# The reciprocal root of a layer norm as one power on GpSimd, and the product with it there too

## The reference, cut to what matters

```python
WIDTH, LAYERS, M1, M2 = (32, 4, 12, 12)
def layer_norm(x, g, b):
    mu = jnp.mean(x, axis=-1, keepdims=True)
    var = jnp.mean((x - mu) ** 2, axis=-1, keepdims=True)
    return (x - mu) * jax.lax.rsqrt(var + EPS) * g + b
h = layer_norm(x @ fc0_w + fc0_b, ln0_g, ln0_b)
for i in range(LAYERS):
    x1 = spectral_conv(h, w1, w2)        # 2-D FFT, 24 x 12 modes mixed over channels, inverse FFT
    x2 = jnp.einsum('bchw,oc->bohw', h, conv_w[i]) + conv_b[i][None, :, None, None]
    h = layer_norm(x1 + x2, ln_g[i], ln_b[i])
    if i < LAYERS - 1:
        h = gelu(h)
h = gelu(h @ fc1_w + fc1_b)
h = gelu(h @ fc2_w + fc2_b)
h = h @ fc3_w + fc3_b
```

## Time and profile before

| | |
|---|---|
| runs | 3285.81, 3277.0, 3279.34 us; median 3279.34 |
| span of the profiled execution | 3279.2 us (an own total of that execution is not listed) |
| TensorE busy | 2937.9 us, 90% of the span |
| VectorE busy | 2145.9 us, 65% |
| ScalarE busy | 1950.3 us, 59% |
| GpSimd busy | 61.9 us, 2% |
| chain that ended last | TensorE 79%, VectorE 11%, issue 5%, ScalarE 5% |
| costliest group of VectorE | reduction of line 1624, 397.0 us in 320 |
| product of line 1638 | 386.8 us in 320 |

### The profile page before, as it was taken

The page is one execution under the profiler, slowest core; times in us unless marked ns, Lnnn a source line. Parts: engine busy times, 40 slices in busy tenths (PEclk is TensorE's granted clock), DMA queues, the critical chain, the costliest instruction groups (busy, mean ns, idle before and its releaser), DMA issues.

```text
span 3279.2 us, 82177 instructions
## 1 busy us (share of the span) xinstructions
PE 2937.9 (90%) x32240; PEld 1867.7 (57%) x32240; DVE 2145.9 (65%) x3954; ACT 1950.3 (59%) x2271; POOL 61.9 (2%) x81
## 2 busy tenths in 40 slices
PE   7888889999889999889999889999999987964994
PEld 3545466666666666666666544444444447952893
DVE  6888668888668888668888644454445434255457
ACT  6777656666556666556666457777777753422451
POOL 0000000000000000000000010000000001000000
PEclk9999999999999999999999999999999998986897
DMA  3422346544447544546544423111111000000000
GB/s 96 130 97 99 100 152 209 193 165 164 152 130 218 183 164 163 155 154 209 179 165 164 151 67 86 46 55 58 46 46 55 29 1 1 1 1 0 1 1 13
DMA packets 98093, 335.91 MB, mean 102 GB/s; under 512 B 29928, under 2 KB 61960, under 8 KB 62088
## 3 DMA queue, kind: packets, MB, share of 16 engines
q1 hardware_dynamic: 75400, 161.50, 16.4%
q10 hardware_dynamic: 18432, 134.23, 10.0%
q0 software_dynamic: 4096, 37.75, 5.3%
HBM read 179.29 MB, written 154.14 MB: 102 GB/s over the span
## 4 chain that ended last, share of the span: by engine, by line
PE 79%; DVE 11%; issue 5%; ACT 5%; DVEq 0%; SPq 0%; DMA 0%; ACTq 0%
PE pA L1291 15%; PE pA L1299 8%; PE pT L1385 8%; PE pT L1317 5%; PE pS L1328 5%; PE pD L1342 4%; PE pD L1374 4%; PE pD L1356 4%; PE pD L467 3%; PE pA L467 3%; PE pD L1263 3%; PE pA L1281 3%; PE pS L459 2%; PE pT L459 2%; DVE arena L1657 2%
## 5 line engine op out<-in xcount | busy, mean ns | idle before, releaser
L1624 DVE TENSOR_REDUCE small<-arena 128x32 f32<-128x1056 f32 x320 | 397.0, 1241 | 316.0 <-ACT arena L1461 311.3
L1291 PEld LDWEIGHTS pA<-conv_bd,h_in 128*128 128x128 f32 x4096 | 479.0, 192 | 109.4 <-issue 92.7
L1291 PE MATMUL pA<-conv_bd,h_in 128*128 128x128 f32 x4096 | 517.4, 280 | 8.6 <-DVE arena L1617 2.9
L1451 ACT COPY w_sb<-pA 128x1024 f32<-128x1024 f32 x256 | 259.8, 1015 | 393.0 <-PE pA L1299 343.3
L1638 DVE SCALAR_TENSOR_TENSOR w_sb<-w_sb,small 128x1024 f32<-128x1024 f32 x320 | 386.8, 1213 | 5.5
L1472 ACT ACTIVATE h_new<-pT,bet,gam 128x1024 f32<-128x1024 f32 x256 | 307.5, 1201 | 100.2 <-PE pT L1317 92.1
L1461 ACT ACTIVATE arena<-w_sb 128x1024 f32<-128x1024 f32 x320 | 339.3, 1060 | 13.4
L1317 PEld LDWEIGHTS pT<-cst,w_sb 128*128 128x128 f32 x2048 | 225.2, 143 | 144.5 <-issue 123.9
L1317 PE MATMUL pT<-cst,w_sb 128*128 128x128 f32 x2048 | 283.0, 282 | 23.2 <-DVE w_sb L1638 23.2
L1476 ACT COPY h_rows<-pS 128x1024 f32<-128x1024 f32 x256 | 257.1, 1004 | 64.9 <-PE pS L1328 64.6
L1328 PEld LDWEIGHTS pS<-cst,h_new 128*128 128x128 f32 x2048 | 228.5, 143 | 113.0 <-issue 71.6
(11 more groups left out here) (299 smaller groups left out, 3903.0 us busy)
## 6 DMA issues: line engine op xcount, KB each, us to landing
h_scratch<-h_new ACTq DMA_DIRECT2D x128, 1024.0 KB, 4.5
h_in<-h_scratch SPq DMA_DIRECT2D x128, 1024.0 KB, 5.1
y_scratch<-w_sb POOLq DMA_DIRECT2D x32, 576.0 KB, 8.4
y_in<-y_scratch SPq DMA_DIRECT2D x512, 36.0 KB
w_sb<-in_L_tok_w1r_dram POOLq DMA_DIRECT2D x8, 576.0 KB, 7.0
w_sb<-in_L_tok_w1i_dram POOLq DMA_DIRECT2D x8, 576.0 KB, 6.7
w_sb<-in_L_tok_w2r_dram POOLq DMA_DIRECT2D x8, 576.0 KB, 8.3
w_sb<-in_L_tok_w2i_dram POOLq DMA_DIRECT2D x8, 576.0 KB, 7.7
```

The lines of the kernel that those rows point to most:

```text
L1291: pe.matmul(pA[:, c:c + 128], h_in[:, 1024 * n + c:1024 * n + c + 128], conv_bd[:], start=(j == 0), stop=False, skip_group_check=True)
L1624: dve.reduce_sum(var[n], sq[n % 2], axis=AX).then_inc(s["summed"], 1)
```

## The change

The seven instructions of `root` go. GpSimd gets `rs` and `scale`: one power of `var` to -0.5 (the exponent is a tensor that holds -0.5 in every place), and one product. Both stand in a new string `POOL` of each stage, in the order of the units, and leave the VectorE strings; nothing else in the strings moves. GpSimd's program is rebuilt so that it follows the bodies: the weight loads, the stores of `y` and the copy into `conv_bd` stand between whole bodies. The clearing of `spec` is cut into two halves, after bodies 2 and 3 of stage last, that of `XT` comes after body 4, and SyncE's `token_params` moves from before group 2 to before group 5 of that stage and waits for both halves. `alone` adds one to a semaphore that nothing waits for.

```diff
@@ ORDER, stage first @@
-        "DVE": ("red.3- rs.3- scale.3- cen.0 cen.1 cen.2 red.0 rs.0 scale.0 red.1 f1.0- rs.1 f1.1- red.2 scale.1 "
-                "f2.0- rs.2 f2.1- scale.2"),
+        "DVE": ("red.3- cen.0 cen.1 cen.2 red.0 red.1 f1.0- f1.1- red.2 f2.0- f2.1-"),
+        "POOL": ("rs.3- scale.3- rs.0 scale.0 rs.1 scale.1 rs.2 scale.2"),
@@ ORDER, stage mid @@
-        "DVE": ("red.3- i1.0 rs.3- scale.3- cen.0 cen.1 i1.1 red.0 rs.0 scale.0 red.1 rs.1 f1.1- scale.1 red.2 f1.0- "
-                "rs.2 f2.0- cen.2 scale.2 f2.1-"),
+        "DVE": ("red.3- i1.0 cen.0 cen.1 i1.1 red.0 red.1 f1.1- red.2 f1.0- f2.0- cen.2 f2.1-"),
+        "POOL": ("rs.3- scale.3- rs.0 scale.0 rs.1 scale.1 rs.2 scale.2"),
@@ ORDER, stage last @@
-        "DVE": ("rs.2- scale.2- turn.1- i1.1 red.3- turn.2- rs.3- scale.3- i1.0 turn.3- red.0 red.1 rs.0 rs.1 red.2 "
-                "scale.0 scale.1 turn.0"),
+        "DVE": ("turn.1- i1.1 red.3- turn.2- i1.0 turn.3- red.0 red.1 red.2 turn.0"),
+        "POOL": ("rs.2- scale.2- rs.3- scale.3- rs.0 scale.0 rs.1 scale.1"),
...
-                def rs(h, g):
-
-                    dve.wait_ge(s["summed"], at("summed", ph, L, g, 1 * h + 1))
-                    alone(dve)
-                    c = slice(32 * h, 32 * h + 32)
-                    root(dve, small[:, 128:256][:, c], small[:, 0:128][:, c], root_x, root_u, s["root_chain"], s["rooted"])
-
-                def scale(n, g):
-
-                    dve.wait_ge(s["rooted"], at("rooted", ph, L, g, n // 1 + 1))
-                    z = raw[n].rearrange("p (x o) -> p x o", x=32)
-                    r = rstd[n].rearrange("p (x o) -> p x o", o=1)
-                    dve.scalar_tensor_tensor(out=z, in0=z, scalar=ROOT_SCALE, in1=r.broadcast_to([P, 32, C]),
-                                             op0=ALU.mult, op1=ALU.mult).then_inc(s["normed"], 1)
...
+            pool.memset(minus_half, -0.5).then_inc(s["halves_set"], 1)
...
+                def rs(n, g):
+
+                    if first_group(g) and ph == "first" and n == 0:
+                        pool.wait_ge(s["halves_set"], 1)
+                    pool.wait_ge(s["summed"], at("summed", ph, L, g, n + 1))
+                    alone(pool)
+                    pool.tensor_tensor(rstd[n], var[n], minus_half, ALU.pow).then_inc(s["rooted"], 1)
+
+                def scale(n, g):
+
+                    pool.wait_ge(s["rooted"], at("rooted", ph, L, g, n + 1))
+                    alone(pool)
+                    z = raw[n].rearrange("p (x o) -> p x o", x=32)
+                    r = rstd[n].rearrange("p (x o) -> p x o", o=1)
+                    pool.tensor_tensor(z, z, r.broadcast_to([P, 32, C]), ALU.mult).then_inc(s["normed"], 1)
...
+            def layer(ph, L, do, prepared):
+
+                bodies(ph, do, 1, 2)
+                if ph == "first":
+                    weights(0, 0, 0)
+                    bodies(ph, do, 2, 3)
+                    weights(0, 0, 1)
+                    bodies(ph, do, 3, 4)
+                    weights(0, 1, 0)
+                    bodies(ph, do, 4, 5)
+                    weights(0, 1, 1)
+                    bodies(ph, do, 5, 5 + 10)
+                else:
+                    mixed(L, 1)
+                    weights(prepared, 0, 0)
+                    bodies(ph, do, 2, 3)
+                    weights(prepared, 0, 1)
+                    bodies(ph, do, 3, 5)
                     y_store(L, 1)
...
+                    bodies(ph, do, 5, 6)
+                    weights(prepared, 1, 0)
+                    bodies(ph, do, 6, 7)
+                    weights(prepared, 1, 1)
+                    bodies(ph, do, 7, 15)
+                y_store(prepared, 0)
+                bodies(ph, do, NG - 1, NG)
+                channel_weights(prepared)
...
+            body("into_last", bound(last, 0), bound(here, NG - 1))
+            bodies("last", last, 1, 2)
+            y_store(LAYERS - 1, 1)
+            bodies("last", last, 2, 3)
+            half = at_col[0] // 2
+            pool.memset(spec[:, 0:half], 0.0).then_inc(s["par_cleared"], 1)
+            bodies("last", last, 3, 4)
+            pool.memset(spec[:, half:at_col[0]], 0.0).then_inc(s["par_cleared"], 1)
+            bodies("last", last, 4, 5)
+            pool.wait_ge(s["normed"], at("normed", "last", LAYERS - 1, 4, 2))
             pool.memset(XT[64:128, :], 0.0).then_inc(s["ones_set"], 1)
...
+            bodies("last", last, 5, NG)
+            body("last", None, bound(last, NG - 1))
             token_pool(pool)
```

More of the change, by code:

```diff
@@ L162 @@
                 "mix.0 fc1.0 fc1.1"),
-        "DVE": ("red.3- i1.1 rs.3- scale.3- i1.0 red.0 rs.0 scale.0 red.1 rs.1 f1.1- scale.1 red.2 f1.0- f2.0- f2.1- "
-                "mix.0 turn.0"),
+        "DVE": ("red.3- i1.1 i1.0 red.0 red.1 f1.1- red.2 f1.0- f2.0- f2.1- mix.0 turn.0"),
+        "POOL": ("rs.3- scale.3- rs.0 scale.0 rs.1 scale.1"),
     },
@@ L1144, in y_store, with steps, mixed, channel_weights @@
                         pool.dma_start(dst, src).then_inc(s["y_stored"], 16)
[L1146 to L1152, removed]
+            def steps(p):
+                ph, L = p.ph, p.L
+                def rs(n, g):
[6 more added lines that the diff above has]
+                    pool.wait_ge(s["rooted"], at("rooted", ph, L, g, n + 1))
+                    alone(pool)
+                    z = raw[n].rearrange("p (x o) -> p x o", x=32)
+                    r = rstd[n].rearrange("p (x o) -> p x o", o=1)
+                    pool.tensor_tensor(z, z, r.broadcast_to([P, 32, C]), ALU.mult).then_inc(s["normed"], 1)
+                return dict(rs=rs, scale=scale)
+            def mixed(L, half):
+                n = 2 * L + half
+                pool.wait_ge(s["mix_a_free"], 3 * n + 3)
+                alone(pool)
+                pool.wait_ge(s["mix_b_free"], 3 * n + 3)
+                alone(pool)
+            def channel_weights(L):
+                if isinstance(L, int) and L == 0:
                     pool.wait_ge(s["conv_chain"], 2)
@@ L1171, in _, with body @@
[L1171 to L1174, removed]
+                    alone(pool)
+                pool.tensor_copy(conv_bd[:], conv_all[:, bass.ds(P * L, P)]).then_inc(s["conv_ready"], 1)
+            def body(order, early, late):
+                for op, n, is_late in parse(ORDER[order]["POOL"]):
+                    do = late if is_late else early
+                    if do:
+                        do[op](n)
@@ new lines, in bound, with bodies @@
+            def bound(do, g):
+                return {op: (lambda n, f=f: f(n, g)) for op, f in do.items()}
+            def bodies(ph, do, first, last):
+                if last - first == 1:
+                    body(ph, bound(do, first), bound(do, first - 1))
+                else:
+                    with pool.Fori(first, last) as b:
+                        body(ph, bound(do, b), bound(do, b - 1))
+            def layer(ph, L, do, prepared):
[9 more added lines that the diff above has]
+                    bodies(ph, do, 5, 5 + 10)
+                else:
+                    mixed(L, 1)
[3 more added lines that the diff above has]
+                    bodies(ph, do, 3, 5)
+                    y_store(L, 1)
+                    bodies(ph, do, 5, 6)
[6 more added lines that the diff above has]
+                channel_weights(prepared)
@@ new lines, in _ @@
+            make = lambda ph, L: steps(Phase(ph, L))
+            first = make("first", 0)
+            body("first", bound(first, 0), None)
+            layer("first", 0, first, 0)
+            body("mid", bound(make("mid", 0), 0), bound(first, NG - 1))
+            with pool.Fori(0, LAYERS - 2) as L:
+                here = make("mid", L)
+                layer("mid", L, here, L + 1)
+                body("mid", bound(make("mid", L + 1), 0), bound(here, NG - 1))
+            L = LAYERS - 2
+            here, last = make("mid", L), make("last", LAYERS - 1)
@@ L1658, in f2 @@
                                   bank.rearrange("p (t n) -> p t n", t=2)[:, :, 0:384]).then_inc(s["d_free"], 1)
[L1660 removed]
+                return dict(cen=cen, i1=i1, red=red, turn=turn, f1=f1, f2=f2)
             phases(dve, "DVE", mix, steps, conv_centre, centring)
```

47 lines of the change are left out of this document (9 added, 38 removed).

## The result

The changed kernel takes **3,660 us** (median; 3,652 to 3,668) where the kernel before takes 3,281.6 (the median of four runs): a ratio of 1.115, with a 95% interval of 1.113 to 1.117. The prediction was 3,266 us, its range ended at 3,325. It is wrong in sign and in size: 378 us slower.

What follows compares the result with a forecast made beforehand. TensorE was taken as the bound, with its waits for VectorE's product to be won. Gains of 8.4 us (first stage) and 4.7 (middle), 13.1 together, off 3,279.2 gave 3,266 us; range 3,256 to 3,325.

Steps and rivals of the forecast that it cites:

- the price p of the power: Time of one GpSimd power over 32 elements a partition, on the path from red to turn: taken as 1.0 us.
- the high bound "from rows": For the power: VectorE's seven root instructions, 1.33 us, times the engines' ratio on a product, 1.88, giving 2.5 us.
- The slower rival: A long power makes the turns wait in first and middle stages: at p = 3.0, 32 us slower, 3,311; chance 0.30.
- Its price formula: Each of 15 first bodies loses p - 1.06, each of some 45 middle ones p - 2.65, against the gain of 13.1 us.
- The gain of a body: First stage: TensorE's turn.2- and a later transpose wait less, 0.56 us a body; middle bodies with centring: 0.13 us.
- The 13.1 us of the sum: Whole saving claimed: 8.4 us in the first stage plus 4.7 us in the middle stage, off 3,279.2.
- the 4.7 us of the middle stages: Middle stage: 36 bodies with centring, each 0.13 us shorter with a lighter VectorE.
- The queues, put at 0: GpSimd's queue: moved y stores, weight loads, conv_bd copy, clears and parameter loads, each taken to cost 0.
- the sign of late weights: Sign that the forecast is wrong: VectorE idle in front of cen.0 at each layer's third body.
- The store of y that I looked at: The y store's four issues stand before rs.3-, whose turn.3- comes five TensorE operations later: cost 0.
- The port: VectorE with two SBUF inputs and GpSimd reading SBUF exclude each other; charged nothing, by that rule 3,281; chance 0.10.
- The rival's form of it: With a power of 1.3 us or more, cen.2 holds scale.3- up, 14.6 us in 12 bodies: about 3,281; chance 0.10.

Runs made afterwards that it cites:

- The halved run: The changed kernel with the power on 16 of the 32 columns, the other roots left at 1.0: 3,298.8 us, ratio 1.0055.
- With p at 0.24: The changed kernel with the power replaced by a product of two constant tiles of the same shape: 3,273.5 us, ratio 0.9969.
- the run with the product alone: The changed kernel with the root back as VectorE's seven instructions, only the product on GpSimd, the root's scale in the squares: 3,288.1 us, ratio 1.0019.

## Why the prediction was wrong

**The step that failed is the price p of the power.** I took 1.0 us and called 2.5 the high bound "from rows". It is 5.43. The bound came from VectorE's seven instructions times the ratio of the engines on a product, so it took for granted that a power is a handful of products. The halved run shows 158 ns an element against 1.9 for the product, over 80 times as much. My other argument, that "one instruction pays its start once", is true and beside the point: the start is 0.38 us. The text said that no row excludes a power in long loops, and then gave that 15% and left it out of the range. With nothing in the trace about an operation, the ratio of other operations is no bound.

**The slower rival had the mechanism, not the size.** It named the place, and its last sentence, that above 3.3 us four units no longer fit a first body, is what happened: 29.9 us against 23.9. Its price formula would give 15 x 4.37 + 45 x 2.78 - 13.1, some 178 us, at p = 5.43. Measured are 382 between the spans. It charged one late unit a body; the runs show all four serial on one engine, and TensorE at the lower clock after many of its stands (125.8 us of the 382).

**The gain of a body was right, the total in part by luck.** With p at 0.24 nine first bodies took 209.2 us instead of 215.3, 0.67 less each (0.56 predicted), and the middle ones fell by the predicted 0.13. The 13.1 us of the sum correspond to a ratio of 0.996, at the edge of the measured interval. But the same run holds two terms that I had put at 0 and that nearly cancel: the first body of the last stage takes 68.26 us instead of 75.31, the second 56.08 instead of 46.96. And the 4.7 us of the middle stages do not show in their sum, 1,362.0 us against 1,360.1 between the first and last red.0 of each; the bodies with the mixes vary by more than that.

**Smaller terms.** The product: 1.91 us, not 2.27; half of one long product of another kind was an over-estimate by a fifth. Red's end to GpSimd's start is 0.18, not 0.24, and power to product 0.18, not 0.1. The last stage's bodies: unchanged in the ten of the table, right, but not in three of the five before them. The first is shorter, with the clears moved out of it. The second waits for the store of y (next paragraph). In the fifth the two clears of XT, 3.51 us each, which I had put at 0, stand on GpSimd in front of a power, and a turn stands 3.71 us for the product behind it; with the power left out the same body takes 47.07 us.

**The queues, put at 0, were not 0.** The loads of the weights, "0 to 2 us a layer", cost 8.8 us in the first stage of the run with the product alone, where the middle stage makes up for most of its own. In the changed kernel VectorE stood 39.1 us in 4 waits before cen.0 for them, the sign of late weights that the prediction names. The store of y that I looked at was the one before turn.3-; the one that hurts is the last, whose landing ScalarE's first fin.0 needs: 8.5 us. I asked who stands behind these DMAs in the queue, not who waits for their landing.

**The port.** I wrote that the rows of before say nothing against running both engines at once. They do, between the first two red.0 of the last stage: 5.97 us instead of 0.18, beside a clear. I had looked beside the one product of 4.54 us only. The Trainium skill's rule that I quoted, VectorE with two SBUF inputs against a GpSimd that reads, agrees with the 1.90 us of line 200. Beside a power, which reads two tensors as well, only one half of it shows. With the power alone on GpSimd, 26 powers that start 0.26 us into a product of VectorE take 6.24 us instead of 5.43, most of the 0.95 us that the product still runs. But in the changed kernel 45 of the 48 cen.2 start during a power and take 0.91 to 1.02 us, where the earlier trace rows has 0.96: a power that started first does not hold them. And the rule does not cover the clear, which reads nothing, nor cen.1 in the changed kernel, a TENSOR_SCALAR of 0.24 us that took 1.06 beside a product. The same section of the Trainium skill ("SBUF — State Buffer", "Who interferes with whom") lists tensor_scalar among the operations that can, when their operands allow it, take both ports of VectorE and so collide with GpSimd; these rows agree. The rival's form of it, cen.2 holding up the product, was not put to the test: in no trace does a product start while cen.2 runs, and none took longer than 1.93 us.

## What to carry to other kernels

An operation that no row shows has no price until it is measured alone: give its long case a chance and a place in the range, above all when the cover is a few microseconds. When work moves to an idle engine, add up the whole body there, all units in a row, and not only one unit's path. And of each DMA that changes its place in a queue, ask who waits for its landing, a stage later too.

## What the runs showed of the hardware

A GpSimd power of two f32 tensors costs 158 ns for each element of a partition (from 16 and 32 of them), and 0.24 us is what a product of the same 128x32 costs. A clear on GpSimd can hold a small VectorE instruction to its own end (0.18 us to 5.97). A power does not do the same to an instruction with two SBUF inputs that starts after it (0.91 to 1.02 us beside powers of 5.43), though it is held itself by such a product that has started before it (6.24 us instead of 5.43). TensorE ran the same eight transposes in 1.97 us, at a granted clock of 0.50, after standing 3.93 us, and in 1.09, at 1.00, after standing 0.42; in the first stage the granted clock fell to 0.86 of full speed in the mean, although the work is the same.
